# A recommendation tower on one Trainium2 core: in the first tile, when the field-row broadcasts and the second tile's gathers are issued, and where in a tile the embedding conversion stands

## The chip, the cores and the metric

The kernel runs on one core of one Trainium2 chip. The metric is the device time of one execution in microseconds (us), lower is better. Before the change the median of three runs is 2730.25 us (2727.2 to 2735.01).

## The reference, cut to what matters

For each of 2048 samples, 39 ids pick 39 embeddings of 16 numbers. They pass a compressed interaction network of three layers (`_L0_rec_ref`), whose outputs are summed over the 16 numbers; 256 sums and 16 dense features then pass a small multilayer perceptron (272 to 512 to 256 to 1).

```python
e = jnp.stack([tbl_0[ids[:, 0]], ..., tbl_38[ids[:, 38]]], axis=1)
# one layer: x0 is e, xk is the half of the last layer's output that goes on
z = jnp.einsum('bhd,bkd,hks->bsd', x0, xk, W) + b[None, :, None]
z = jax.nn.relu(z)
xk = z[:, :half, :]
direct.append(z[:, half:, :])
# at the end
logit = jnp.sum(jnp.concatenate(direct, axis=1), axis=-1)
```

## The kernel before, in words

**Tiles and chunks.** A tile is 128 samples (16 tiles), and a tile has four chunks of 4 of the 16 embedding numbers, so a chunk is 512 columns. Per tile GpSimd (POOL) gathers 39 embeddings per sample with 39 indirect DMAs (`gather_tile`, L294 to L304) into `emb`. ScalarE (ACT) and VectorE (DVE) convert `emb` into a rounded high part and a remainder (`high_emb` L317, `low_emb` L494, `full_emb` L323) in `emb2`; TensorE (PE) transposes the quarter that a chunk needs (`transposes` L598). ACT copies the transposed rows out of PSUM twice (`copy_x` L328): into `rows_sb`, from which SyncE (SP) writes the chunk's 39 rows to a scratch in DRAM (`write_rows` L233), and into `x2`.

**Layer 0** uses sums of pairs, their squares, and a contraction: seven rounds of `sums` (PE L607), `square` (ACT L337), `contract0` (PE L612). PE and ACT take turns over two PSUM banks, `aux_ready` going from PE to ACT and `aux_read` back. The result becomes `xk1` (`next_field`, L348 and L349).

**Layers 1 and 2** are 20 steps per chunk, numbered k: k 0 to 9 belong to layer 1 and k 10 to 19 to layer 2. Each step takes a pair of field rows, broadcast over 64 partitions each, multiplies it with `xk` on DVE (`product`, L485, 128x1024), and contracts the product on PE. Twelve of the 20 steps are split: ACT rounds the product (L341), DVE forms the remainder (`low`, L490), and PE contracts in three parts (L629, L633). The other eight are plain (L621). The products go through a ring of `RING = 4` buffers, so DVE can be four steps ahead of PE.

**The pairs of rows** come from `spread(c, p)` (L240): two broadcast DMAs of 256 KB each from the DRAM scratch to slot `x_slot(c, p)` of `xb`. Ten pairs serve a chunk, in layer 1 and again in layer 2. The four pairs p < `PRE` = 4 have slots for two chunks, the others one slot. Layer 1 of a chunk starts four steps early: its first four steps are k 6 to 9 of the chunk before, and for chunk 0 of tile 0 a prologue.

**What sets the order.** Each engine runs an instruction list written out by hand, and waits on semaphores. All broadcasts and scratch writes are on SP's one queue. In `tile` (SP, L257) a chunk first writes the rows of the chunk two ahead, and then issues pair p when the product of step k = 10 + p of the chunk has been made. The prologue of SP (L252 to L255) is written as follows:

```python
for c in range(2):
    write_rows(0, c)
    for p in range(PRE if c else PAIRS):
        spread(c, p)
```

So the ten pairs of chunk 0 are issued with no wait between them, and `write_rows(0, 1)` and four pairs of chunk 1 stand behind them. On POOL, `gather_tile(0)` is followed by a loop that waits for `emb2_ready` (the end of the conversion of the tile before) and gathers the next tile; so the gathers of tile 1 start when `full_emb(0)` has ended. PE's and ACT's prologues run layer 0 for group 0 and group 1 (the first two chunks), and inside group 1 the first four steps of chunk 0 (`contract(0, s, ...)`, with `round_` on ACT L369 and the loop of DVE from L516).

**The conversion** of the next tile stands in chunk 1 of every tile but the last, at steps `HIGH_AT, LOW_AT, FULL_AT = 4, 6, 8` (L39): ACT's `high_emb` ahead of its work of step 4, DVE's `low_emb` ahead of step 6, ACT's `full_emb` ahead of step 8. The transposes that need it are at step 0 of chunk 2. Also placed by step number are ACT's `direct2` (3), `next_field` and `direct1` (9), `direct0` (16), `next_field` of layer 0 (19), and DVE's folds, four additions at steps 5 to 8 of chunk 0 and at 12 to 15 of chunk 3.

Of the kernel before, what the change touches and what calls it, by code (L numbers as in the profile page):

```python
# [26 lines left out]
PAIRS = T1 // 2  # L27


PRE = 4  # L30
# [5 lines left out]
SUM_AT = [3, 5, 7, 9, 11, 12, 14]  # L36
SQUARE_LAG, CONTRACT_LAG = 2, 3
RELU2_AT, RELU1_AT, DIRECT0_AT, RELU0_AT = 3, 9, 16, 19
HIGH_AT, LOW_AT, FULL_AT = 4, 6, 8  # L39
FOLD1_AT, FOLD0_AT = 5, 12  # L40
FOLDS = 4
SPL = sorted(SPLIT)
# [12 lines left out]
def step_no(c, k, end=False):  # L55

    return PRE + STEPS * c + k - (PRE if end and k >= L2 else 0)
# [7 lines left out]
def x_slot(chunk, p):  # L65

    return PRE * (chunk % 2) + p if p < PRE else PRE + p


def field(t, j):  # L70

    return NF - 1 if t == SINGLE else 2 * t + j - (2 if t > SINGLE else 0)
# [7 lines left out]
def build(nc, ids, tables, x0_dram, sel0_d, inc_d, w0a_d, w0b_d, w1_d, w2_d, b_d, dense_d, wt1_d, wx_d, bt1_d, wt2_d, bt2_d,  # L80
          wt3_d, out):
    ctx = ExitStack()
    with ctx:
# [6 lines left out]
        def sem(name):  # L90
            return ctx.enter_context(nc.semaphore(name))
# [81 lines left out]
        products = sem("products")  # L173
# [29 lines left out]
        def dram_pair(k):  # L203

            if k >= L2:
                return w2_d[:, 2 * (k - L2):2 * (k - L2) + 2, :]
            p = (k + PRE) % PAIRS
            return w1_d[:, 2 * p:2 * p + 2, :]
# [13 lines left out]
        @block.sync  # L222
        def _(sp):
            sp.dma_start(ids_sb[:, :, :], ids.rearrange("(t p) f -> p t f", p=TB)).then_inc(ids_in, 16)
            for dst, src in ((w0a_st, w0a_d), (w0b_st, w0b_d), (inc, inc_d), (sel0_st, sel0_d),
                             (bias[:, :], b_d), (wt3[:, :], wt3_d), (bt1[:, :], bt1_d), (bt2[:, :], bt2_d)):
                sp.dma_start(dst, src).then_inc(weights_in, 16)
            for q, k in enumerate(SPL):
                sp.dma_start(w_st[:, q], dram_pair(k)).then_inc(weights_in, 16)
            for q, k in enumerate(PLAIN):  # L230
                sp.dma_start(wp[:, q], dram_pair(k)).then_inc(weights_in, 16)

            def write_rows(T, c):  # L233

                sp.wait_ge(rows_ready, T * CPT + c + 1)
                sp.dma_start(x0_dram[c % SCRATCH, 0:NF, :], rows_sb[:, c % 2, :]).then_inc(rows_written, 16)
                sp.wait_ge(rows_written, 16 * (T * CPT + c + 1))
                sp.sem_inc(rows_settled, 1)

            def spread(c, p):  # L240

                q = x_slot(c, p)
                for j in range(2):
                    h, h2 = field(2 * p, j), field(2 * p + 1, j)
                    src = x0_dram[c % SCRATCH, h:h2 + 1:h2 - h, :]
                    sp.dma_start(xb[j * K1:(j + 1) * K1, q, :, :], src.unsqueeze(0).broadcast_to([K1, 2, N]))\
                        .then_inc(xb_in[q], 16)


            sp.wait_ge(weights_made, 6)  # L250
            sp.wait_ge(parts_made, 2)
            for c in range(2):  # L252
                write_rows(0, c)
                for p in range(PRE if c else PAIRS):
                    spread(c, p)  # L255

            def tile(T, last=False):  # L257
                for c in range(CPT):
                    if not (last and c >= 2):
                        write_rows(T, c + 2)  # L260
                    if last and c == CPT - 1:
                        continue
                    for p in range(PAIRS):
                        if last and c == 2 and p < PRE:
                            continue

                        sp.wait_ge(products, T * PER["step"] + step_no(c, L2 + p) + 1)
                        spread(c + 2 if p < PRE else c + 1, p)

            with sp.Fori(0, TILES - 1) as T:  # L270
                tile(T)
            tile(TILES - 1, last=True)


            sp.wait_ge(products, PRE + all_steps - STEPS)
            sp.dma_start(wt1, wt1_d[0:256, :].rearrange("(t p) n -> p t n", p=128)).then_inc(mlp_in, 16)
            sp.dma_start(wt2, wt2_d.rearrange("(t p) n -> p t n", p=128)).then_inc(mlp_in, 16)
            sp.dma_start(wx_st, wx_d).then_inc(mlp_in, 16)

            sp.wait_ge(products, all_steps - (PAIRS - PRE))  # L280
            sp.dma_start(dense_st, dense_d).then_inc(dense_in, 16)
            sp.wait_ge(m3_read, BATCH // N)
            sp.dma_start(out.rearrange("(a n) o -> a (n o)", a=1), y_sb).then_inc(out_done, 16)
            sp.wait_ge(out_done, 16)

        @block.gpsimd
        def _(pool):
            pool.memset(ident[:, :], 0.0).then_inc(idx_ready, 1)
            pool.wait_ge(idx_ready, 1)
            pool.affine_select(out=ident[:, :], in_=ident[:, :], compare_op=ALU.not_equal, fill=1.0, base=0,  # L290
                               pattern=[[-1, 128]], channel_multiplier=1).then_inc(idx_ready, 1)
            pool.wait_ge(ids_in, 16)

            def gather_tile(T):  # L294
                pool.sem_inc(settled, 1)
                pool.tensor_copy(idx[:, :], ids_sb[:, bass.ds(T, 1), :].rearrange("p a f -> p (a f)"))\  # L296
                    .then_inc(idx_ready, 1)
                pool.wait_ge(idx_ready, T + 3)
                pool.sem_inc(settled, 1)
                for f in range(NF):  # L300
                    pool.indirect_dma_start(emb[:, f, :], None, tables[f],  # L301
                                            bass.IndirectOffsetOnAxis(ap=idx[:, f:f + 1], axis=0))\
                        .then_inc(gathered, 16)
                pool.wait_ge(gathered, (T + 1) * (16 * NF))  # L304

            gather_tile(0)
            with pool.Fori(1, TILES) as T:
                pool.wait_ge(emb2_ready, T)
                gather_tile(T)
# [492 lines left out]
```

## Time and profile before

| | us |
|---|---|
| median of 3 runs | 2730.25 |
| the profiled execution | 2730.05 |
| its span | 2728.2 |
| PE busy | 2597.3 (95% of the span) |
| DVE busy | 2471.9 (91%) |
| ACT busy | 1475.9 (54%) |
| POOL busy | 960.2 (35%) |
| 16 DMA engines, queue of SP | 59.3% of their span |

The profiled execution lies 0.2 us under the median, and its span 1.9 us under its own time. Lines such as L485 are lines of the kernel before. In the rows below, "SPq" is the issuing of DMAs by SP; a bracket holds the idle time of the engine ahead of the row and what ended it. "remote" or "another core or an unknown queue" is a semaphore wait whose releaser the profile could not name, and "issue" is time in which the profile shows nothing that the engine waited for. Matmul ends are modelled.

### The profile page before, as it was taken

The page shows a single profiled execution, that of the slowest core. Times are in us where ns is not written, and L with a number is a line of the kernel's source. Part 1 is how long each engine was busy: PE and PEld are TensorE (multiplying, and loading weights), DVE is VectorE, ACT ScalarE, POOL GpSimd, SP SyncE. Part 2 cuts the span into 40 slices and gives each one's busy share as a digit, 9 for nine tenths or more (in the row PEclk, how much of TensorE's full clock was granted, in tenths as well). Part 3 has the DMA queues.
Part 4 walks back from the last instruction along what each step waited for, and adds up shares of the span by engine and source line. Part 5 has one row for each costly group of instructions (what it writes and reads, how often), then busy time and mean ns, then how long its engine had stood idle before and what let it go on. Part 6 is the DMA issues. An engine that isn't in the chain of part 4 may idle for free.

```text
span 2728.2 us, 29051 instructions
## 1 busy us (share of the span) xinstructions
PE 2597.3 (95%) x8334; PEld 1521.9 (56%) x8334; DVE 2471.9 (91%) x2206; ACT 1475.9 (54%) x1863; POOL 960.2 (35%) x646
## 2 busy tenths in 40 slices
PE   1599999999999999999999999999999999999989
PEld 0255565555555555565555555555655555555545
DVE  1299999999999999999999999999999999999991
ACT  1255555655555555555556555555655555555543
POOL 6527071542707153260805326080533608000000
PEclk9799999999999999999999999999999999999999
DMA  2556665675667567566756766675576657556730
GB/s 69 113 117 128 152 140 120 138 159 119 129 147 143 122 132 159 125 131 140 150 122 126 158 129 133 133 156 123 126 151 140 131 124 160 124 126 141 155 77 1
DMA packets 214669, 352.43 MB, mean 129 GB/s; under 512 B 34373, under 2 KB 47546, under 8 KB 214546
## 3 DMA queue, kind: packets, MB, share of 16 engines
q1 hardware_dynamic: 194675, 346.95, 59.3%
q0 software_dynamic: 19968, 5.15, 1.7%
q8 instruction: 14, 0.23, 0.0%
q14 instruction: 12, 0.10, 0.0%
HBM read 346.86 MB, written 5.12 MB: 129 GB/s over the span
## 4 chain that ended last, share of the span: by engine, by line
PE 50%; DVE 23%; issue 15%; DMA 5%; ACT 3%; POOL 1%; another core or an unknown queue 1%; DVEq 1%; SPq 1%; ACTq 0%; POOLq 0%
PE ps L621 16%; PE ps L629 12%; DVE P L485 11%; PE ps L612 9%; DVE Pl L490 9%; PE ps L633 8%; DMA xb<-x_dram 5%; DVE dir L512 2%; PE ps L607 2%; POOL emb L301 1%; ACT Ph L341 1%; PE ps L728 1%; PE ps L718 1%; DVE emb L496 1%
## 5 line engine op out<-in xcount | busy, mean ns | idle before, releaser
L485 DVE TENSOR_TENSOR P<-xb,xk 128x1024 f32<-128x1024 f32 x1280 | 1532.9, 1220 | 48.5 <-issue 21.8
L341 ACT ACTIVATE Ph<-P 128x1024 fp32r<-128x1024 f32 x768 | 807.0, 1057 | 441.9 <-DVE P L485 427.2
L490 DVE TENSOR_TENSOR Pl<-P,Ph 128x1024 fp32r<-128x1024 f32 x768 | 939.2, 1223 | 95.0 <-ACT Ph L341 69.6
L301 POOL DMA_INDIRECT emb<-tbl_in,idx x624 | 883.0, 1415 | 230.2 <-issue 217.0
L621 PE MATMUL ps<-P,wp 128*128 128x512 f32 x2048 | 962.7, 597 | 0.0
L629 PE MATMUL ps<-Ph,wh 128*128 128x512 f32 x1536 | 794.9, 517 | 6.7 <-ACT Ph L341 6.7
L621 PEld LDWEIGHTS ps<-P,wp 128*128 128x128 f32 x2048 | 383.4, 190 | 342.2 <-issue 301.2
L629 PE MATMUL ps<-Ph,wl 128*128 128x512 f32 x1408 | 556.0, 395 | 0.0
L633 PE MATMUL ps<-Pl,wh 128*128 128x512 f32 (+1 forms) x1536 | 517.1, 410 | 30.5 <-DVE Pl L490 28.9
L337 ACT ACTIVATE sq<-ps 117x512 f32<-117x512 f32 (+1 forms) x448 | 264.9, 591 | 459.9 <-PE ps L607 340.3
L612 PE MATMUL ps<-sq,w 117*128 117x512 f32 (+1 forms) x896 | 472.0, 608 | 20.5 <-ACT sq L337 11.3
L296 POOL COPY idx<-ids_sb 128x39 int32 (+1 forms) x16 | 76.6, 4785 | 1131.2 <-ACT emb L325 1127.8
L629 PEld LDWEIGHTS ps<-Ph,wh 128*128 128x128 f32 x1536 | 291.2, 190 | 194.0 <-issue 135.8
L633 PEld LDWEIGHTS ps<-Pl,wh 128*128 128x128 f32 (+1 forms) x1536 | 275.5, 188 | 178.8 <-DVE Pl L490 88.3
L629 PEld LDWEIGHTS ps<-Ph,wl 128*128 128x128 f32 x1408 | 267.7, 190 | 147.1 <-issue 108.2
L607 PE MATMUL ps<-x,sel 78*117 78x512 f32 (+1 forms) x448 | 258.3, 577 | 9.8 <-issue 8.6
L612 PEld LDWEIGHTS ps<-sq,w 117*128 117x128 f32 (+1 forms) x896 | 166.6, 192 | 148.6 <-issue 119.5
L348 ACT ACTIVATE xk<-ps,bias 64x512 f32<-64x512 f32 x128 | 86.7, 677 | 115.8 <-PE ps L612 64.2
L607 PEld LDWEIGHTS ps<-x,sel 78*117 78x117 f32 (+1 forms) x448 | 78.9, 177 | 68.7 <-issue 55.5
L331 ACT ACTIVATE rows_sb<-ps 39x512 f32<-39x512 f32 x64 | 37.9, 592 | 129.4 <-PE ps L600 123.7
L349 ACT ACTIVATE xk<-ps,bias 64x512 f32<-64x512 f32 x128 | 87.3, 682 | 1.6
L600 PE MATMUL ps<-ident,emb 128*78 128x128 f32 x256 | 38.9, 275 | 39.8 <-ACT emb L325 39.8
(53 smaller groups left out, 509.3 us busy)
## 6 DMA issues: line engine op xcount, KB each, us to landing
xb<-x_dram SPq DMA_DIRECT2D x1280, 256.0 KB
emb<-tbl_in,idx POOLq DMA_INDIRECT x624
x_dram<-rows_sb SPq DMA_DIRECT2D x64, 78.0 KB
xb<-w_in SPq DMA_DIRECT2D x12, 128.0 KB
wp<-w_in SPq DMA_DIRECT2D x8, 128.0 KB
xb<-wt_in SPq DMA_DIRECT2D x2, 512.0 KB, 7.1
xb<-dense_in SPq DMA_DIRECT2D x1, 768.0 KB, 5.2
xb<-w0a_in SPq DMA_DIRECT2D x1, 409.5 KB
```

What stands on the lines that cost most here:

```text
L301: pool.indirect_dma_start(emb[:, f, :], None, tables[f], bass.IndirectOffsetOnAxis(ap=idx[:, f:f + 1], axis=0))\
L337: act.activation(sq[0:rows, t % 2, :], aux_ps[0:rows, number % 2, :], ACT.Square).then_inc(aux_read, 1)
L341: act.activation(Ph[:, s % RING], P[:, s % RING], ACT.Copy).then_inc(rounded, 1)
L348: act.activation(xk[lo, :], z[lo], ACT.Relu, bias=b[lo])
L349: act.activation(xk[hi, :], z[lo], ACT.Relu, bias=b[lo]).then_inc(ready, 1)
L485: dve.tensor_tensor(P[:, s % RING], xb[:, slot], xk.unsqueeze(1).broadcast_to([128, 2, N]), ALU.mult)\
L490: dve.tensor_tensor(Pl[:, s % RING], P[:, s % RING], Ph[:, s % RING], ALU.subtract)\
L607: pe.matmul(aux_ps[0:rows, number % 2, :], sel[:, t, 0:rows], x2[0:R2, slot, :], start=True, stop=True)\
L612: m = pe.matmul(z0_ps[bank], w0[0:rows, t, :], sq[0:rows, t % 2, :], start=t == 0, stop=t == T0 - 1)
L621: m = pe.matmul(z, wp[:, PLAIN.index(k), j, :], P[:, s % RING, j, :], start=start and j == 0, stop=stop and j == 1)
L629: pe.matmul(z, w[:, q, j, :], Ph[:, s % RING, j, :], start=start and i + j == 0, stop=False)
L633: m = pe.matmul(z, wh[rows, q, j, :], Pl[rows, s % RING, j, :], start=False, stop=stop and j == 1)
```

## The change

It has three parts.

1. **SP's prologue.** The rows of chunk 0 are written, pairs 0 to 3 of chunk 0 are issued, then the rows of chunk 1 are written; pairs 4 to 9 of chunk 0 follow, each behind a wait for one more product (1 to 6), and pairs 0 to 3 of chunk 1, each behind a wait for one more (7 to 10).
2. **POOL.** Ahead of the loop that gathers tiles 1 to 15 there is a wait for the first product.
3. **The conversion** in chunk 1 of every tile but the last moves from steps 4, 6, 8 to steps 11, 13, 15.

```diff
-HIGH_AT, LOW_AT, FULL_AT = 4, 6, 8
+HIGH_AT, LOW_AT, FULL_AT = 11, 13, 15
...
-            for c in range(2):
-                write_rows(0, c)
-                for p in range(PRE if c else PAIRS):
-                    spread(c, p)
+            write_rows(0, 0)
+            for p in range(PRE):
+                spread(0, p)
+            write_rows(0, 1)
+            for p in range(PRE, PAIRS):
+                sp.wait_ge(products, p - PRE + 1)
+                spread(0, p)
+            for p in range(PRE):
+                sp.wait_ge(products, PAIRS - PRE + p + 1)
+                spread(1, p)
...
             gather_tile(0)
+            pool.wait_ge(products, 1)
             with pool.Fori(1, TILES) as T:
                 pool.wait_ge(emb2_ready, T)
                 gather_tile(T)
```

## Rows read from the trace of the kernel before

**Rows 1.** The page: PE's busy tenths in 40 slices; the group of the gathers

```profile
PE   1599999999999999999999999999999999999989
...
L301 POOL DMA_INDIRECT emb<-tbl_in,idx x624 | 883.0, 1415 | 230.2 <-issue 217.0
```

**Rows 2.** Chain that ended last, 55 to 150 us: start, length, what

```profile
64.68 1.20 PE ps L607 x2
...
76.93 0.68 ACT xk L348
...
78.30 5.65 another core or an unknown queue
...
86.69 1.48 another core or an unknown queue
...
88.80 5.75 issue
...
96.09 7.37 another core or an unknown queue
...
105.02 14.58 another core or an unknown queue
...
129.03 0.68 ACT xk L348
```

**Rows 3.** Timeline of PE around those waits: start, length, instruction

```profile
75.90 0.60 PE L600 MATMUL ps<-ident,emb 128*78 128x128 f32 x4
...
89.97 1.42 PE L607 MATMUL ps<-x,sel 78*117 78x512 f32 x1
...
99.06 0.40 PE L607 MATMUL ps<-x,sel 78*117 78x512 f32 x1
...
108.57 0.41 PE L607 MATMUL ps<-x,sel 78*117 78x512 f32 x1
```

**Rows 4.** By stretch: length, busy PE, PEld, DVE, ACT, POOL; PEclk, DMA share, GB/s

```profile
86.00:90.00 4.00, 3.56 (x7) 1.46 (x6) 0.00 (x0) 1.19 (x2) 3.08 (x4) 0.50 1.07 213
...
110.00:114.00 4.00, 0.00 (x0) 0.00 (x0) 0.00 (x0) 0.00 (x0) 2.74 (x3) 0.75 0.08 6
...
154.00:175.00 21.00, 21.00 (x71) 12.58 (x70) 19.44 (x17) 10.23 (x13) 0.00 (x0) 1.00 1.05 226
```

**Rows 5.** Timeline of SP's DMA issues in tile 0: start, length, instruction

```profile
64.25 0.33 SPq L236 DMA_DIRECT2D x_dram<-rows_sb  x1
66.14 13.54 SPq L246 DMA_DIRECT2D xb<-x_dram  x20
84.59 0.33 SPq L236 DMA_DIRECT2D x_dram<-rows_sb  x1
93.99 9.44 SPq L246 DMA_DIRECT2D xb<-x_dram  x8
...
151.50 18.62 SPq L246 DMA_DIRECT2D xb<-x_dram  x20
```

**Rows 6.** Chunks 1, 2, 3 of one middle tile, then chunk 1 of the last; columns as above

```profile
1126.25:1165.52 39.27, 39.05 (x128) 23.15 (x127) 38.01 (x34) 24.32 (x30) 22.09 (x12) 1.00 0.63 133
1165.52:1204.41 38.89, 38.89 (x128) 23.16 (x127) 37.23 (x33) 22.02 (x28) 24.60 (x19) 1.00 0.69 140
1204.41:1243.19 38.78, 38.78 (x129) 23.30 (x128) 37.72 (x36) 22.00 (x28) 15.85 (x11) 1.00 0.70 144
2551.18:2589.95 38.77, 38.77 (x129) 23.37 (x127) 36.53 (x33) 22.01 (x28) 0.00 (x0) 1.00 0.63 141
```

**Rows 7.** Timeline of DVE and of PE in that middle tile's chunk 1

```profile
1132.35 1.22 DVE L496 TENSOR_TENSOR emb<-emb 128x624 f32<-128x624 f32 x1
...
1149.53 1.26 DVE L490 TENSOR_TENSOR Pl<-P,Ph 128x1024 fp32r<-128x1024 f32 x1
...
1153.14 0.62 PE L633 MATMUL ps<-Pl,wh 128*128 128x512 f32 x2
```

**Rows 8.** Timeline of POOL: the copy of indices ahead of that tile's gathers

```profile
1139.56 5.44 POOL L296 COPY idx<-ids_sb 128x39 int32 x1 [84.49 <-ACT emb L325]
```

## The prediction

> **What bounds the kernel now.** I read the page's slices first, to see where PE, the busiest engine, is not full [rows 1]: from the third slice (a slice is 68 us) to the end it is at nine tenths, and only the first two slices and the very end are lower. PE's work is the same before and after, so there are two places to look: the start, and the small losses of the full stretch.
>
> The start I read in the chain of waits [rows 2]. The reader is to see five pieces between 78.30 and 119.60 us in which no instruction runs on the chain: 5.65, 1.48, 5.75, 7.37 and 14.58 us, 34.8 us in all. Each ends with an instruction of ACT that waits for `aux_ready` from PE. PE had long issued what it waits for [rows 3]: the transposes stand at 75.90 while ACT goes on only at 83.95; the sum of 89.97 is taken up at 103.46, that of 99.06 at 119.60. So PE's signal, or ACT's notice of it, comes many us late, and group 1 takes 50.7 us from 78.30 to the row at 129.03. Group 0, with the same seven rounds, took 12.3 us from 64.68 to 76.93 [rows 2].
>
> What is peculiar to this stretch? At 86 us the DMA engines are full at 213 GB/s [rows 4]. But they are as full in 154 to 175 us, and there PE is busy 21.00 of 21.00 us. The difference is in the queue of SP [rows 5]: here 20 broadcasts are issued in 13.54 us, and the row write at 84.59, behind them, lands only when the next broadcast starts at 93.99. From 66.14 to 93.99 is 27.85 us for 20, or 1.39 us each, so at 79.7 some ten wait in the queue. In steady state 20 are issued over 18.62 us. The gathers of tile 1 run beside them (POOL is busy in both stretches of the start, and not at 154). In the longest hole, at 110 to 114, the broadcasts are gone and only gathers run, at 6 GB/s [rows 4]. So rows point to two suspects, the deep queue and the gathers, and the change thins both.
>
> The full stretch I read by chunks [rows 6]. Chunk 1 of a middle tile takes 39.27 us, chunk 2 38.89, chunk 3 38.78. Chunk 1 of the last tile, which has no conversion, takes 38.77. So 0.50 us of chunk 1 goes with the conversion, in 15 tiles. DVE spends 1.22 us on `low_emb` at 1132.35 [rows 7], ahead of the four split steps 5 to 8, and PE's idle time in that chunk is 39.27 - 39.05 = 0.22 us; the rest shows as matmuls that start later than they could.
>
> **The change part by part.** *SP's prologue.* It removes nothing; twenty-eight broadcasts and two row writes stay. What it moves: the row write of chunk 1 goes from behind 20 broadcasts to behind 8. Eight take 8 x 1.39 = 11.1 us, 66.14 to 77.3, and ACT's rows are there at about 79, so that write no longer queues; a row write alone takes 66.14 - 64.25 = 1.9 us [rows 5]. What it adds: ten waits on SP. The pair for product n (n from 5 to 14) waits for product n - 4, so three products lie between issue and need. The price of a pair, from the rows: 1.9 us for a transfer's round trip and 2 x 1.39 us for the bytes, 4.7 us, and at most 6.0 if its two issues (13.54 / 20 = 0.68 us each) are not covered at all. Three products in the full stretch take 3 x 38.8 / 20 = 5.8 us. I take 4.7, since a pair issued alone has nothing ahead of it, and so put these waits at nothing; the cover is 1.1 us thick. The first four (pairs 4 to 7) are released by the four products of the prologue, long before use. Behind the last wait (product 10) stands the row write of chunk 2; its first reader is the pair released by product 15, five steps or 9.7 us later, against 1.9 us and four pairs of backlog at most, so that costs nothing either.
>
> *POOL.* The gathers of tile 1 start behind product 1, which follows the 78.30 us of the chain [rows 2] by one product of DVE, so at about 80 us, instead of right behind `full_emb(0)`, ahead of 64.68. A tile's 39 gathers take 39 x 1.415 = 55.2 us and their gaps of 0.3 us some 12 [rows 1], behind a copy of at most 5.44 us [rows 8], so they end near 153. The conversion that needs them now stands at step 11 of chunk 1: chunk 0 starts near 99, a chunk lasts at least 38.8, and 11 steps at 1.94 are 21 more, 159 us. So I put this at nothing; it matters through what it takes out of the start.
>
> *The start, summed.* If the holes go, group 1 costs what is left. From below: 50.7 - 34.8 = 15.9 us, if all that PE did under the holes was free. From above: PE worked under three of the holes, from 88.80 to 91.39, 96.09 to 99.46 and 105.02 to 108.98 [rows 3], 9.9 us, which gives 25.8. Group 0 is the nearest row: 12.3 us, with 1.1 for ACT's copies ahead of it, and four contractions on top, of which a chunk's mean is below 1.94 us (38.8 / 20): 21.2. I take 21, for a gain of 50.7 - 21 = 29.7 us (24.9 to 34.8). PE's granted clock was 0.50 of full, the 1.2 GHz level, at 86 to 90 us, after it had idled; a shorter idle may keep the higher level, which I leave in the range.
>
> *The conversion.* Same instructions, other places. What leaves: 0.50 us x 15 = 7.5 us. What comes: at step 13 DVE's remainder is ready at 1149.53 + 1.26 = 1150.79 and PE takes it up at 1153.14 [rows 7], a slack of 2.35 us, more than the 1.22 us of `low_emb`. And chunk 3 carries four folds on DVE at steps 12 to 15 (DVE 37.72 us, with PE full at 38.78 of 38.78) at no cost [rows 6]. ACT's two conversions are 24.32 - 22.02 = 2.3 us in a chunk in which it is busy 24.32 of 39.27. So nothing comes back: gain 7.5 (bounds: 7.5, and a loss of 1.2 a tile if that slack were not there). The gathers of the next tile start seven steps, 13.6 us, later; they leave chunk 1 and reach further into chunk 3. Chunk 2, which has most of them, is 0.12 us over the floor, so I put the shift at nothing, within 0.3 us a tile, 4.5 us either way.
>
> The sum against the profiled execution's own time: 2730.05 - 29.7 - 7.5 = 2692.9, and the median lies 0.2 above it: 2693.
>
> **A rule against the change.** The rows show full DMA engines beside a full PE at 154 us, and full DMA engines beside an ACT that stands still from 88.80 to 94.55 [rows 2, 4]. The Trainium skill (SBUF — State Buffer, "Who interferes with whom") says that DMA never contends with a compute engine and that "PE and ACT never wait on anyone". By that rule the holes aren't made by transfers and thinning them removes nothing; the stretch at 154 us agrees with it, that at 86 does not settle it.
>
> **The rivals.** *The holes stay.* Their cause is something else in this stretch, such as the first pass through the code or the clock; for it speaks that the longest one has idle DMA engines [rows 4], against it that group 0, also a first pass, has none. Only the conversion gains: 2730.25 - 7.5 = 2722.8. The Trainium skill's page SBUF — State Buffer, in the rule above, leads to this case; the trace bears it out at 154 us only, so it has a small chance.
>
> *Half of the holes stay*, because the gathers make them: they still run beside group 1, from 80 us on. For it speaks the 14.58 us hole with gathers alone; against it the middle tiles, where gathers run beside a full PE [rows 6]. 2693 + 34.8 / 2 = 2710.
>
> *The new place costs.* The holes go, but `full_emb` and `low_emb` among steps 13 to 15 take 1.2 us a tile from PE: 2693 + 7.5 + 15 x 1.2 = 2719.
>
> *Slower.* SP's waits are too tight: the lead of three products isn't there, as DVE makes products faster than PE's mean once it has slots, and with ten pairs each waiting the whole 4.7 us DVE stands 47 us. It decides where a pair's landing passes the time of three products. With the gains it ends at 2693 + 47 = 2740, slower than before. If only the excess of 6.0 over 5.8 is lost it is 2 us. Against it: DVE is bounded by PE through the ring of four.
>
> *Less is changed than said.* The waits could be met already when SP comes to them. For pairs 4 and 5 that is so (products 1 and 2 are made at once); for the others not, since product 3 comes behind a rounding in group 1. The short name speaks of the first tile alone, but the third part acts in 15 tiles; it is in the sum.
>
> **How the numbers follow.** Holes gone and conversion free: 0.62, 2693, with 2684 (34.8 us gained, and some of the gathers' 4.5) to 2701. Half the holes: 0.13, 2710. New place costs: 0.06, 2719. Holes stay: 0.12, 2723. Slower: 0.07, around 2740. The likeliest gives 2693. The range reaches over the first three, 2684 to 2720, and leaves out 0.19. A change of under 0.3%, 8.2 us, is about what a measurement here can't tell from none, so faster means under 2722.1 and slower over 2738.4. Faster: the first three and some of the fourth, 0.84. Same: most of the fourth and part of the last, 0.11. Slower: 0.05.
>
> **What would show it.** Right: the chain has no piece named as unknown over 2 us after 78 us; the row `next_field` of group 1 stands near 99 instead of 129.03; middle chunks 1 take 38.8 us. Pair by pair: DVE waits for xb in tile 0 by under 1 us each. Wrong: holes of the old length with PE's sums long done (the cause is another), holes of half the length beside gathers, PE waiting for a remainder at steps 13 to 16 of chunk 1, or DVE's products in chunk 0 of tile 0 each waiting for a broadcast.

## The result and the profile after

The changed kernel takes 2681.49 us, median of 4 runs (2679.7 to 2683.57); the kernel before, run beside it, takes 2728.9 (2727.2 to 2735.01). The ratio is 0.9822, with a 95% interval of 0.9807 to 0.9838: faster by 47 us, which is clear of the noise though under 2%. The forecast was 2693 with a range of 2684 to 2720, so the sign was right and the size was outside the range, 2.5 us below its lower end.

The profiled execution took 2682.74 us, with a span of 2680.9. First the page of the kernel after, as in [rows 1]: PE's slices, and the group of the gathers (busy us, mean ns, idle us ahead).

```profile
PE   0999999999999999999999999999999999999989
...
L307 POOL DMA_INDIRECT emb<-tbl_in,idx x624 | 949.7, 1522 | 226.1 <-issue 212.8
```

The second slice has gone from 5 tenths to 9. The gathers cost more each, 1522 ns for 1415 in [rows 1], and nothing on the chain waits for it. The chain of waits of the kernel after, in the stretch of [rows 2] (start, length, what):

```profile
77.34 0.68 ACT xk L356
78.04 0.59 ACT rows_sb L338
...
79.17 0.79 PE ps L614
79.98 0.60 ACT sq L344
...
93.83 1.72 PE ps L628 x4
95.55 0.86 PE ps L619 x2
...
96.85 2.82 issue
```

Between 78 and 96.4 us no piece is named "unknown" any more: ACT and PE hand over to each other, and `next_field` of group 1 begins at 96.44 where it began at 129.03. The timeline of the kernel after, SP's issues in tile 0 and this row of ACT (start, length, instruction, idle time ahead of it):

```profile
66.23 5.22 SPq L246 DMA_DIRECT2D xb<-x_dram  x8
...
78.66 0.33 SPq L236 DMA_DIRECT2D x_dram<-rows_sb  x1
80.50 28.25 SPq L246 DMA_DIRECT2D xb<-x_dram  x20
...
96.44 0.68 ACT L355 ACTIVATE xk<-ps,bias 64x512 f32<-64x512 f32 x1 [2.85 <-PE ps L619]
...
108.98 0.39 SPq L236 DMA_DIRECT2D x_dram<-rows_sb  x1
```

The burst of [rows 5] is now 8 broadcasts, then the row write, which lands in 1.84 us (78.66 to 80.50), then 20 broadcasts over 28.25 us. The four chunks of the middle tile (columns of [rows 4]):

```profile
1045.68:1086.79 41.11, 39.86 (x128) 22.84 (x127) 40.74 (x38) 22.03 (x28) 0.00 (x0) 1.00 0.60 134
1086.79:1125.57 38.78, 38.78 (x129) 23.32 (x128) 37.85 (x34) 24.50 (x30) 9.47 (x7) 1.00 0.63 133
1125.57:1164.34 38.77, 38.77 (x128) 23.30 (x127) 37.17 (x33) 22.01 (x28) 32.67 (x21) 1.00 0.68 138
1164.34:1203.11 38.77, 38.77 (x128) 23.30 (x127) 37.85 (x36) 22.11 (x28) 21.59 (x14) 1.00 0.69 137
```

Against [rows 6], chunk 1 has lost 0.49 us and chunk 2 0.12; over all tiles chunk 2 lost 0.26 on average. The chunks' lengths over all tiles, from the starts of PE's transposes in the two timelines, divide the whole difference of the spans:

| | before, us | after, us | gained |
|---|---|---|---|
| start of the first full chunk | 128.83 | 96.25 | 32.6 |
| chunks 0, sum | 661.2 | 659.7 | 1.5 |
| chunks 1 | 589.3 | 581.6 | 7.7 |
| chunks 2 | 585.6 | 581.6 | 4.0 |
| chunks 3 | 586.3 | 584.8 | 1.5 |
| end | 177.06 | 177.04 | 0.0 |
| sum | | | 47.3 |

Two thirds of the gain is at the start, one third in the steady state (how much of that third a second pair of profiles repeats is told below). The row of 41.11 us is worth a look as well: chunk 0 is 2.3 us longer than the others, before and after.

### The profile page after: what moved, and what is told of

Same layout as the page of the kernel before. It is cut to its first block, busy times and chain, and to the rows that moved or that the text cites. A ratio compares the mean times of both kernels' runs of the same rounds, so it can differ in the third digit from the quotient of the medians.

```text
span 2680.9 us, 29052 instructions
## 1 busy us (share of the span) xinstructions
PE 2582.5 (96%) x8334; PEld 1524.9 (57%) x8334; DVE 2468.8 (92%) x2206; ACT 1480.1 (55%) x1863; POOL 967.0 (36%) x646
## 4 chain that ended last, share of the span: by engine, by line
PE 69%; DVE 15%; issue 9%; DMA 4%; POOL 1%; ACT 1%; DVEq 0%; SPq 0%; ACTq 0%; POOLq 0%
PE ps L628 24%; PE ps L636 18%; PE ps L619 12%; PE ps L640 10%; DVE P L492 7%; DVE Pl L497 5%; DMA xb<-x_dram 4%; PE ps L614 3%; DVE dir L519 2%; POOL emb L307 1%; PE ps L735 1%; PE ps L725 1%; PE ps L607 1%; ACT Ph L348 0%; SPq L246 0%
## 5 line engine op out<-in xcount | busy, mean ns | idle before, releaser
L307 POOL DMA_INDIRECT emb<-tbl_in,idx x624 | 949.7, 1522 | 226.1 <-issue 212.8
L302 POOL COPY idx<-ids_sb 128x39 int32 (+1 forms) x16 | 16.6, 1038 | 1096.1 <-ACT emb L332 1070.4
```

What stands on the lines that cost most here:

```text
L307: pool.indirect_dma_start(emb[:, f, :], None, tables[f], bass.IndirectOffsetOnAxis(ap=idx[:, f:f + 1], axis=0))\
```

## The experiments

One thing has to be known ahead of the numbers. The kernel before was run on seven occasions, the comparison above among them. It took about 2730 us on three (2728.9, 2731.66, 2731.80) and about 2697 on the other four (2697.47, 2698.42, 2696.06, 2699.93); its runs of one occasion lie within 9 us. The same chip number stands on record for 2698.42 and for 2731.80, so the chip alone doesn't decide it. Each measurement is read against the kernel before of its own occasion. "The waits" below are the five pieces of [rows 2], which the prediction calls holes, and waits like them. The edits are cut, and shown against the kernel after; the column of parts says what else a run has. "Start" is the time at which chunk 0's first full pass begins in the profile, in us.

| run | parts of the change, folds | this, us | before beside it | ratio (95%) | start |
|---|---|---|---|---|---|
| sp_only | 1 | 2698.61 | 2697.47 | 1.0003 (0.9994 to 1.0013) | 96.34 |
| pool_only | 2 | 2700.54 | 2697.47 | 1.0009 (1.0000 to 1.0019) | 94.12 |
| steps_only | 3 | 2683.79 | 2697.47 | 0.9944 (0.9927 to 0.9960) | 93.91 |
| order_only | 1, no SP waits | 2697.80 | 2697.47 | 0.9999 (0.9989 to 1.0008) | 92.38 |
| before_again | none | 2698.52 | 2698.42 | 0.9997 (0.9987 to 1.0006) | 94.1 |
| after_again | 1, 2, 3 | 2684.44 | 2698.42 | 0.9940 (0.9923 to 0.9956) | 95.87 |
| late_gathers | 1, 2, gathers held | 2694.33 | 2698.42 | 0.9984 (0.9974 to 0.9994) | 94.07 |
| fold12 | 1, 2, 3, folds 12 | 2656.14 | 2698.42 | 0.9838 (0.9822 to 0.9854) | 94.07 |
| oldstart_fold14 | 3, folds 14 | 2652.99 | 2696.06 | 0.9842 (0.9824 to 0.9860) | 94.65 |
| sp_steps_fold12 | 1, 3, folds 12 | 2654.83 | 2696.06 | 0.9845 (0.9829 to 0.9862) | 94.57 |
| pool_steps_fold12 | 2, 3, folds 12 | 2655.02 | 2696.06 | 0.9848 (0.9831 to 0.9864) | 96.00 |
| sp_steps_fold14 | 1, 3, folds 14 | 2680.86 | 2731.66 | 0.9817 (0.9788 to 0.9845) | 122.77 |
| pool_steps_held | 2, 3, folds 14, gathers held | 2654.45 | 2731.66 | 0.9720 (0.9692 to 0.9748) | 93.9 |
| gath_rows | gathers at 68 us, 3, folds 12 | 2654.42 | 2699.93 | 0.9834 (0.9805 to 0.9862) | 94.13 |
| gath_split | 13 gathers at 63 us, 3, folds 12 | 2653.36 | 2699.93 | 0.9830 (0.9801 to 0.9859) | 94.0 |
| gath_rows_b | as gath_rows | 2654.09 and 2691.01 | 2731.80 | 0.9786 (0.9707 to 0.9864) | 94.22 |
| best | 2, 3, folds 14 | 2654.20 | 2731.80 | 0.9719 (0.9703 to 0.9736) | 93.2 |

### One part at a time

**sp_only**: the change's part 1 alone.

```diff
-HIGH_AT, LOW_AT, FULL_AT = 11, 13, 15
+HIGH_AT, LOW_AT, FULL_AT = 4, 6, 8
...
-            pool.wait_ge(products, 1)
```

> The kernel before with part 1 alone (SP's prologue with its ten waits); gathers of tile 1 start at once, conversion at 4, 6, 8. Theory A (the holes come from the deep queue of broadcasts): all five holes go, next_field of group 1 at 96 to 98 us, time 32 us under before, about 2697. Theory B (the gathers make them): half or more of the 34.8 us stay, next_field of group 1 at 110 us or later, time 2712 or more. Chunks 1, 2 and 3 stay at 39.28, 39.03 and 39.06 us in both.

**pool_only**: part 2 alone, with SP's prologue of the kernel before.

```diff
-HIGH_AT, LOW_AT, FULL_AT = 11, 13, 15
+HIGH_AT, LOW_AT, FULL_AT = 4, 6, 8
...
-            write_rows(0, 0)
-            for p in range(PRE):
...
+            for c in range(2):
+                write_rows(0, c)
+                for p in range(PRE if c else PAIRS):
+                    spread(c, p)
```

> The kernel before with part 2 alone (POOL waits for product 1); 20 broadcasts still issued in one burst. Theory A: the holes stay within a few us, next_field of group 1 after 120 us, time 2725 to 2730. Theory B: they go wholly or mostly, time about 2697 to 2712. A hole of 14.58 us that had gathers alone beside it should at least shrink if gathers have a part in it.

**steps_only**: part 3 alone; SP's and POOL's lines as before.

```diff
-            pool.wait_ge(products, 1)
...
+            for c in range(2):
+                write_rows(0, c)
+                for p in range(PRE if c else PAIRS):
+                    spread(c, p)
```

> The kernel before with part 3 alone (conversion at 11, 13, 15). The start is that of before (next_field of group 1 at 129 us). The prediction's term was 7.5 us in chunk 1 and nothing elsewhere: 2722. The trace of after shows 7.7 in chunk 1, 4.0 in chunk 2, 1.5 each in chunks 3 and 0; if all of that is this part's, the time is 2730 - 14.7 = 2715, and chunk 2 is at 38.77 us.

**order_only**: the row write of chunk 1 goes ahead of pairs 4 to 9, but no pair waits for a product.

```diff
             for p in range(PRE, PAIRS):
-                sp.wait_ge(products, p - PRE + 1)
                 spread(0, p)
             for p in range(PRE):
-                sp.wait_ge(products, PAIRS - PRE + p + 1)
                 spread(1, p)
```

> The kernel before with SP's prologue reordered (row write of chunk 1 ahead of pairs 4 to 9) but with no waits for products; POOL and conversion as before. The 20 broadcasts of pairs 4 to 9 and of chunk 1 are now issued in one burst at about 80 us. Theory A in the form 'a burst of 20 is too deep': the holes come back, perhaps later by one group, and the time is within 10 us of before. Theory A' (what hurts is the row write queued behind the burst, with SP standing at its wait): holes go, about 2697. Theory B: as before.

On this occasion the kernel before took 2697.47 us, and no profile of the four has the waits: chunk 0 starts at 92.4 to 96.3 us in all of them. So these runs say nothing on what removes the waits. They say what is left without them: parts 1 and 2 and the mere order of SP gain nothing (1.0003, 1.0009, 0.9999), and part 3 alone gains 13.7 us. pool_only has a cost of its own in tile 0: its conversion at step 4 of chunk 1 waits for gathers that begin late, and that chunk takes 42.88 us instead of 39.3. Parts 2 and 3 belong together.

### Both kernels again, and where the steady state gains

**before_again**: the kernel before, without an edit, with a profile of its own.

> The kernel before, unchanged, with a profile of this occasion. The runs of before beside sp_only, pool_only, steps_only and order_only took 2697.5 us, 33 under the first ones. Theory C: the five holes at 78 to 120 us do not belong to the kernel but come and go with the occasion; where before takes 2697, its group 1 ends near 94 to 96 us, with no wait by an unknown releaser over 1 us, and where it takes 2730 the holes are there. Theory A or B (the program's own queue or gathers make them every time): the holes are in this profile too, and the time is 2728 to 2732.

It took 2698.52 us, as the kernel before beside it. Its timeline, SP's issues and a row of ACT:

```profile
66.22 13.16 SPq L246 DMA_DIRECT2D xb<-x_dram  x20
79.42 0.56 SPq L236 DMA_DIRECT2D x_dram<-rows_sb  x1
...
94.30 0.68 ACT L348 ACTIVATE xk<-ps,bias 64x512 f32<-64x512 f32 x1 [2.85 <-PE ps L612]
94.41 5.12 SPq L246 DMA_DIRECT2D xb<-x_dram  x8
```

and its stretch of [rows 4]:

```profile
86.00:90.00 4.00, 4.00 (x16) 2.65 (x15) 3.74 (x5) 2.04 (x3) 3.08 (x4) 1.00 1.06 215
```

This is the most telling profile of the study. The queue is as deep as in [rows 5], 20 broadcasts in 13.16 us with the row write behind them for 15 us; the DMA share is 1.06 at 215 GB/s; four gathers run beside it. And PE is busy 4.00 of 4.00 us at a clock of 1.00, where in [rows 4] it had 3.56 at 0.50, and group 1 ends at 94.30 instead of 129.03. So neither the deep queue nor the full DMA engines make the waits by themselves, and the late row write costs nothing. The gathers of tile 1 run beside group 0 here too, from 63.68 us, so on this occasion they don't make the waits either.

**after_again**: the changed kernel, without an edit.

> The kernel after, unchanged, on the same chip as before_again. Theory C: 2680 to 2684 as the first time, since its start has no holes either way; the ratio to before is 0.994 (15 us) where before takes 2697. Theory A or B: ratio 0.982.

2684.44, 3 us over its first time, beside a before that is 30 us under its own. Chunks 1 and 2 take 38.77 us again, and chunk 0 starts at 95.87, 1.8 us *later* than in before_again. That isn't the change's: late_gathers and fold12 below have the same start program and begin chunk 0 at 94.07. What differs is the granted clock in group 1. It is 0.50 at 80 to 84 us and 0.70 at 84 to 86 in after_again, and in before_again 0.54 and 0.61 at 80 to 84 and 1.00 from 84. The change's worth is 14 us where the waits don't occur (0.9940), and 47 where they do.

**late_gathers**: the changed kernel with the conversion back at steps 4, 6, 8, while the gathers of tiles 2 to 15 are held until the product of step 15 of chunk 1. It parts the two things that part 3 moves.

```diff
-HIGH_AT, LOW_AT, FULL_AT = 11, 13, 15
+HIGH_AT, LOW_AT, FULL_AT = 4, 6, 8
...
             pool.wait_ge(products, 1)
-            with pool.Fori(1, TILES) as T:
+            pool.wait_ge(emb2_ready, 1)
+            gather_tile(1)
+            with pool.Fori(2, TILES) as T:
                 pool.wait_ge(emb2_ready, T)
+                pool.wait_ge(products, T * PER["step"] - 120)
                 gather_tile(T)
```

> The kernel after, but with the conversion back at 4, 6, 8, and the gathers of tiles 2 to 15 held until the product of step 15 of chunk 1 (about where full_emb ends in after). Splits part 3 into its two effects. If the conversion's place gives chunk 1's 0.5 us a tile and the later gathers give chunk 2's 0.27: chunk 1 at 39.28, chunk 2 at 38.77, time 7.5 us over after plus some 3.5 for gathers of tile 1 that are late for step 4: 2692. If chunk 2's gain is DVE's lead from the new place: chunk 2 at 39.03, 2696. If chunk 1's 0.5 us is the gathers': chunk 1 at 38.77.

Its chunks 1, 2 and 3 of the middle tile:

```profile
1092.44:1131.78 39.34, 39.10 (x129) 23.16 (x128) 38.00 (x34) 24.29 (x30) 10.79 (x8) 1.00 0.63 134
1131.78:1170.55 38.77, 38.77 (x128) 23.31 (x127) 37.03 (x33) 22.01 (x28) 32.67 (x21) 1.00 0.69 138
1170.55:1209.67 39.12, 39.12 (x129) 23.08 (x128) 37.65 (x36) 21.98 (x28) 18.97 (x13) 1.00 0.68 141
```

Chunk 1 is back at 39.3 although the gathers are late, and chunk 2 stays at 38.8 although the conversion is early. So the half microsecond of chunk 1 belongs to the place of the conversion, and what chunk 2 gained belongs to the later gathers. The waits of DVE from 130 to 2507 us (us in total, times, longest) point the same way. In before_again and in after_again:

```profile
DVE P L485 <- DMA xb<-x_dram: 30.3, 51, 1.4
```

```profile
DVE P L492 <- DMA xb<-x_dram: 12.8, 22, 1.5
```

DVE's waits for broadcasts fall from 30.3 to 12.8 us (21.5 to 7.5 in the first pair of profiles), and to 15.2 in late_gathers, with later gathers alone. steps_only, with part 3 alone, has 13.4. In the kernel before the gathers of the next tile begin at step 8 of chunk 1, beside the burst of its later pairs; that this overlap is what lengthens DVE's waits is argued, not shown.

### The folds

Chunk 0, at 41.11 us with DVE at 40.74, has four folds of DVE at steps 5 to 8, the same kind of place from which the change took `low_emb`. **fold12** puts them at steps 12 to 15; the rest is the changed kernel.

```diff
-FOLD1_AT, FOLD0_AT = 5, 12
+FOLD1_AT, FOLD0_AT = 12, 12
```

> The kernel after with the folds of chunk 0 moved from steps 5 to 8 to steps 12 to 15, where chunk 3 has its own at no cost. Chunk 0 takes 41.0 us against 38.8 for chunks 1 and 2, with PE waiting for remainders at steps 5 to 8. By the same reading as for the conversion: chunk 0 falls to 38.8 to 39.0 in 15 tiles, 30 to 34 us, time 2648 to 2652. If chunk 0's excess is not the folds' (the loop's branch, or broadcasts of the chunk before): it stays at 41.0 and the time at 2681.

Its chunks 0 and 1 of the middle tile:

```profile
1037.02:1076.01 38.99, 38.99 (x128) 23.04 (x127) 38.99 (x37) 22.11 (x28) 0.00 (x0) 1.00 0.61 137
1076.01:1114.98 38.97, 38.97 (x128) 23.16 (x127) 38.97 (x34) 24.62 (x30) 9.36 (x7) 1.00 0.63 135
```

2656.14, 28.3 us under after_again. All chunks 0 together go from 660.8 to 629.2 us, a gain of 31.6, and chunks 1 give back 2.5 (581.6 to 584.1), where DVE is now busy without a pause. [rows 6] show 38.77 us as the length of an undisturbed chunk; chunk 0 is 0.2 over it now. The prediction used four folds at steps 12 to 15 of chunk 3 as proof that late steps have slack, and overlooked the four in chunk 0 that stood at early ones.

### Which part removes the waits

**oldstart_fold14**: part 3 with folds at step 14, SP and POOL as before.

```diff
-FOLD1_AT, FOLD0_AT = 5, 12
+FOLD1_AT, FOLD0_AT = 14, 12
...
+            for c in range(2):
+                write_rows(0, c)
+                for p in range(PRE if c else PAIRS):
+                    spread(c, p)
...
-            pool.wait_ge(products, 1)
```

> The kernel before with part 3 and with chunk 0's folds at steps 14 to 17; SP's and POOL's starts as before. If the start parts cost 1.8 us where there are no holes (chunk 0 began at 94.1 us in before_again and at 95.9 in after_again): 1 to 2 us under fold12's 2656, and if steps 14 to 17 hide the folds fully (fold12: chunk 0 at 38.97, chunk 1 at 38.93, floor 38.77), another 5 us: 2649 to 2655. If before takes 2730 on this occasion, theory C2 (the occasion and the old start together make the holes) gives this kernel them too: 2682 to 2688; theory C1 (the occasion alone, whatever the start, and after was lucky) gives them to all three kernels of this call or to none.

**sp_steps_fold12**: the changed kernel without part 2, folds at 12.

```diff
-FOLD1_AT, FOLD0_AT = 5, 12
+FOLD1_AT, FOLD0_AT = 12, 12
...
-            pool.wait_ge(products, 1)
```

> Parts 1 and 3 and the folds at 12; POOL's start as before. Without holes: 2655 to 2657, as fold12. If before takes 2730 here: theory A (queue) no holes, 2656; theory B (gathers) holes, 2672 or more.

**pool_steps_fold12**: without part 1, folds at 12.

```diff
-FOLD1_AT, FOLD0_AT = 5, 12
+FOLD1_AT, FOLD0_AT = 12, 12
...
+            for c in range(2):
+                write_rows(0, c)
+                for p in range(PRE if c else PAIRS):
+                    spread(c, p)
```

> Parts 2 and 3 and the folds at 12; SP's start as before. Without holes: 2654 to 2657; chunk 0 starts at 94.1 us if the 1.8 us are the waits of SP, at 95.9 if they are those of POOL. If before takes 2730 here: theory A holes, 2672 or more; theory B none, 2656.

2652.99, 2654.83 and 2655.02: again an occasion without the waits, and the three can't be told apart. So they don't say which part removes the waits; they repeat that the start is worth nothing then. The next two came on an occasion on which the kernel before took 2731.66.

**sp_steps_fold14**: parts 1 and 3, folds at 14.

```diff
-FOLD1_AT, FOLD0_AT = 5, 12
+FOLD1_AT, FOLD0_AT = 14, 12
...
-            pool.wait_ge(products, 1)
```

> Parts 1 and 3, the folds of chunk 0 at 14 to 17; POOL's start as before. If before takes 2697 here: 2652 to 2656. If it takes 2730: theory A (holes need the burst of broadcasts of the old start) 2652 to 2656, theory B (they need the gathers of tile 1 beside group 1) 2670 or more with holes in the chain after 78 us.

**pool_steps_held**: parts 2 and 3, folds at 14, and the gathers of tiles 2 to 15 held to step 4 of chunk 2.

```diff
-FOLD1_AT, FOLD0_AT = 5, 12
+FOLD1_AT, FOLD0_AT = 14, 12
...
+            for c in range(2):
+                write_rows(0, c)
+                for p in range(PRE if c else PAIRS):
+                    spread(c, p)
...
+            pool.wait_ge(emb2_ready, 1)
+            gather_tile(1)
+            with pool.Fori(2, TILES) as T:
                 pool.wait_ge(emb2_ready, T)
+                pool.wait_ge(products, T * PER["step"] - 111)
                 gather_tile(T)
```

> Parts 2 and 3, folds at 14 to 17, and the gathers of tiles 2 to 15 held until step 4 of chunk 2, when the broadcasts of chunk 1's second half have landed. Chunk 3 is still 0.2 us over the floor in after, with DVE waiting for broadcasts that ran beside gathers. If only overlap with a burst counts: chunk 2's burst and chunk 3's are now beside gathers, so chunk 3 stays at 39.0 and chunk 0 rises by 0.2: 2656. If before takes 2730 here: theory A 2670 or more with holes, theory B none.

2680.86 against 2654.45: 26 us between them, and their starts are 122.77 and 93.9. Chain of sp_steps_fold14 (start, length, what):

```profile
76.35 2.12 issue
...
82.10 2.72 issue
...
92.03 21.52 another core or an unknown queue
...
115.11 3.44 another core or an unknown queue
...
122.97 0.68 ACT xk L354
```

Its timeline, rows of POOL, SP, PE and ACT:

```profile
63.42 0.96 POOL L307 DMA_INDIRECT emb<-tbl_in,idx  x1 [0.81 <-POOL idx L302]
...
65.96 5.26 SPq L246 DMA_DIRECT2D xb<-x_dram  x8
...
79.95 41.14 SPq L246 DMA_DIRECT2D xb<-x_dram  x12
...
95.10 0.39 PE L613 MATMUL ps<-x,sel 78*117 78x512 f32 x1
...
113.57 0.60 ACT L343 ACTIVATE sq<-ps 117x512 f32<-117x512 f32 x1 [21.54 <-remote]
114.22 2.07 PE L618 MATMUL ps<-sq,w 117*128 117x512 f32 x2 [18.72 <-issue]
```

PE's sum stands at 95.10, and ACT squares its result at 113.57: the picture of [rows 3], with SP's queue as shallow as the change makes it, and gathers from 63.42 on. The trace also has the moment at which PE's signal arrives. The sum ends at 95.50, the event of its semaphore stands at 113.55, and ACT goes on 0.02 us later; in before_again such an event stands 0.01 to 0.02 us behind the matmul's end. So it is the signal that is late, not ACT's notice of it. And the timeline of pool_steps_held, rows of SP, POOL and ACT:

```profile
66.20 13.02 SPq L246 DMA_DIRECT2D xb<-x_dram  x20
...
80.04 0.97 POOL L301 DMA_INDIRECT emb<-tbl_in,idx  x1 [0.81 <-POOL idx L296]
...
94.10 0.68 ACT L352 ACTIVATE xk<-ps,bias 64x512 f32<-64x512 f32 x1 [2.85 <-PE ps L616]
```

The old burst of 20, gathers from 80.04 on, and no wait. The two kernels differ in SP's prologue and in the hold of later tiles as well, but all four pairings of the two parts are on record for the three occasions. With gathers from 63 us the waits are there under the old prologue (the kernel before) and under the new one (sp_steps_fold14); with gathers from 80 us or later they are gone under both (the kernel after; this run, and best below without the hold). So on such an occasion POOL's line removes the waits, and SP's part neither removes them nor is needed. The hold itself gains nothing: chunk 2 is short already, and chunk 0 is 39.12 us.

**gath_rows** lets the gathers of tile 1 begin once the first row write has landed, at 67.7 us, so inside group 0. **gath_split** issues 13 of them at once, from 63.5 us, and 26 behind product 1. Both have part 3, folds at 12 and SP's old prologue.

```diff
-            pool.wait_ge(products, 1)
+            pool.wait_ge(rows_settled, 1)
```

> pool_steps_fold12 with POOL waiting not for product 1 (about 78 us) but for the first row write to have landed (about 66 us): the gathers of tile 1 start some 3 us later than before's 62.6 and run through half of group 0 and all of group 1. Where before takes 2697: 2653 to 2657. Where it takes 2730: if any start during group 0 brings the holes, 2670 or more; if only gathers that begin before PE's group 0 do, 2655.

```diff
+                    if split and f == 13:
+                        pool.wait_ge(products, 1)
...
-            pool.wait_ge(products, 1)
+            gather_tile(1, split=True)
```

> pool_steps_fold12 with the first 13 gathers of tile 1 issued at once (62.6 to 79 us) and the other 26 behind product 1. In the first trace of before the first hole began at 78.3, with the 13th gather. Where before takes 2697: 2653 to 2657. Where it takes 2730: if gathers in group 0 bring the holes later on, 2670 or more; if it takes an unbroken row of more than 13, 2655.

2654.42 and 2653.36 beside a before of 2699.93: once more an occasion without the waits, so nothing is told on them. **gath_rows_b** is gath_rows again.

> gath_rows once more, for an occasion on which before takes 2730: 2670 or more if gathers that start in group 0 bring the waits, 2655 if they don't. Where before takes 2697: 2653 to 2657, and nothing is learned.

This time the kernel before took 2731.80, and the two executions took 2654.09 and 2691.01 us. The profile is that of the first. It has one short wait of the kind, in its chain (start, length, what):

```profile
84.36 2.74 another core or an unknown queue
...
87.12 0.60 ACT sq L338
```

The sum that ACT squares there ends at 85.21, and its signal comes at 87.10. The second execution, 37 us longer, was not profiled. So a start of the gathers inside group 0 still lets PE's signals come late; that the 37 us are such waits is an inference from their size.

**best**: parts 2 and 3 with folds at steps 14 to 17, SP as before.

```diff
-FOLD1_AT, FOLD0_AT = 5, 12
+FOLD1_AT, FOLD0_AT = 14, 12
...
+            for c in range(2):
+                write_rows(0, c)
+                for p in range(PRE if c else PAIRS):
+                    spread(c, p)
```

> Parts 2 and 3, chunk 0's folds at 14 to 17, SP's old start: the version to keep. 2651 to 2656 whatever before takes, since POOL's part is enough against the waits of the start and the old SP start was 1.3 us faster in oldstart_fold14 and sp_steps_fold12 (chunk 0 at 94.6 us).

2654.20 (2653.12 to 2655.22), 77.6 us under the kernel before of that occasion: it beats both kernels, and it has no new wait on SP. Its chunks 0 and 1:

```profile
1033.81:1072.81 39.00, 39.00 (x129) 23.09 (x128) 39.00 (x37) 22.19 (x28) 0.00 (x0) 1.00 0.64 138
1072.81:1111.82 39.01, 39.01 (x129) 23.21 (x128) 39.01 (x34) 24.60 (x30) 9.29 (x7) 1.00 0.64 132
```

Its gathers of tile 1 are issued from 80.7 to 146 us, beside most of group 1 and of chunk 0, and its start is at 93.2. So gathers beside matmuls don't make the waits as such; the waits come with gathers that begin ahead of or beside group 0, on some occasions.

## Why the prediction was right and wrong

**The holes go** (right, by the wrong part). The chain has no unknown piece from 78 us on, as the first mark for "right" asked. But the prediction named two suspects and leaned on the deep queue of SP. before_again has that queue and no holes, and sp_steps_fold14 has the shallow queue and holes. The gathers were the second suspect, and moving them was what helped. The rival that blamed them expected half of the holes to stay, since gathers still run beside group 1; none stayed, so what counts is when they begin, not that they run beside it. Two other causes that the prediction named don't hold. No packet of an instruction queue is in the trace of the kernel before from 68 to 127 us, so no code was loaded under the holes. And the granted clock was still 1.00 at 78 to 80 us, when the first hole began, and fell behind it; before_again has 0.54 at 80 to 82 and no hole.

**What group 1 costs without holes** (a term mis-sized). "I take 21, for a gain of 50.7 - 21 = 29.7 us". Group 1 took 18.4 us, from 78.04 to 96.44, so 32.6 us were gained at the start, inside the bounds of 24.9 to 34.8. The four contractions were priced at a mean step, 7.8 us together; in the chain after they take 5.9 us, three of 1.38 and the last of 1.72 (93.83), and the rest of group 1 takes 12.5 us where 13.4 was put. PE didn't keep its clock: in the kernel after it idled for 2.12 us ahead of 79.17, and was granted 0.50, the 1.2 GHz level, at 80 to 84 us, 0.58 at 84 to 86 and 1.00 from 86. In order_only and best it was 1.00 all through, and chunk 0 started at 92.38 and 93.2.

**That the holes belong to the kernel** (not seen). All rows came from one profile. Four of seven occasions have no holes, and no row of a single profile could have told that. The change is worth 14 us on one kind of occasion and 47 on the other. That the comparison fell on the second kind, as the profile before had, is luck: on the first kind the forecast of 2693 would have stood beside a kernel before of 2697 and a kernel after of 2684.

**SP's waits cost nothing** (right). DVE's products of chunk 0 in tile 0 don't wait for a broadcast, and the pairs of 80.50 to 108.75 keep ahead. The slower rival (0.07) had no part. The 1.8 us by which after_again starts later than before_again aren't theirs, as the two runs with the same start program at 94.07 show.

**The row write** (right). It no longer queues, and as before_again shows, its queueing had cost nothing.

**The gathers of tile 1** (right). They ran from 81.3 to 144.6 us, forecast 80 to 153, ahead of step 11 of chunk 1. pool_only shows the cover that the prediction named: with the conversion at step 4 that chunk is 3.6 us longer. The copy ahead of the gathers had a median of 5.44 us before [rows 8] and has 1.12 after.

**The conversion** (right in size). 7.5 us was forecast for chunk 1, and 7.7 came; late_gathers shows that it is its place. Nothing came back at steps 11 to 15: PE is busy 38.78 of 38.78 us.

**The later gathers** (the step that failed). "Chunk 2, which has most of them, is 0.12 us over the floor, so I put the shift at nothing". One middle tile stood for fifteen: over all tiles chunk 2 was 0.26 over the floor, and 4.0 us came from there. It repeats: the chunks 2 sum to 585.6 and 585.7 us in the two profiles of the kernel before, and to 581.6 and 581.8 in the two after. Chunks 3 and 0 gave 1.5 each in this pair of profiles, but two profiles of one kernel differ as much there (chunks 3: 586.3 and 587.7 before, 584.8 and 585.9 after; chunks 0 after: 659.7 and 660.8), so those 3.0 us aren't shown to be the change's. With 2.9 more from the start and 0.2 from chunk 1 this is 10.1 us more than the sum of the prediction; its sum said 2693, and the profiled execution took 2682.74. So two terms failed in size, the shift of the gathers (0 for 4.0) and group 1 (21 for 18.4), both inside their own bounds. The lower end of the range, 2684, took the start's bound whole and the gathers' only in part, and had nothing for chunks 3 and 0.

**The rule against the change.** By the Trainium skill's rule (SBUF — State Buffer, "Who interferes with whom"), DMA never contends with a compute engine. That agrees with before_again, where PE is busy all 4.00 us beside full DMA engines. The prediction drew from it that thinning would remove nothing; that step failed, since the later start of the gathers did remove the waits. The rule itself isn't refuted: it and its sentence "PE and ACT never wait on anyone" are about ports of SBUF, and what ACT waited for was a signal of PE, up to 18.1 us behind the end of the matmul (sp_steps_fold14).

**What stays open.** What delays PE's signals. In sp_steps_fold14 the last gather is issued at 111.88 and the long wait ends at 113.57; in the first profile the last gather is at 112.4 and the last wait ends at 119.60. The ends stand near each other, but they don't name a mechanism. Nor do the runs say what makes an occasion one or the other. One mark of it is in the traces. In the six of the three occasions with the waits, those of the kernel after and of best among them, 456 to 483 events of PE's `aux_ready` are recorded where PE signals 512 times; in the thirteen others it is 505 to 513. So on such an occasion records of signals are missing even where no signal is late, and whether late signals and missing records have one cause, the recording itself included, no run here shows.

## What to carry to other kernels

Look in an unrolled schedule for small operations that stand ahead of a run of the most demanding steps, and move them to where slack is: here 0.5 us per tile for one conversion and 2 for four additions, 36 us together, more than the whole stall at the start. Before a start-up stall is costed, profile the unchanged kernel on another occasion: here it was there three times in seven, and a gain of 47 us is 14 without it. Try a later start for the bulk gathers of a later tile: here they cost up to 33 us when they began beside the first stage, on some occasions, and 4 us when they began seven steps earlier in chunk 1.

## What the runs showed of the hardware

The same program took 2697 or 2730 us by occasion, with its runs of one occasion within 9 us of each other, and the difference is about that of the waits for PE's signals between 78 and 120 us. On the occasions with the waits, they were in both profiles whose gathers begin at 63 us (the kernel before, sp_steps_fold14), a single short one of 2.76 us in the profile whose gathers begin at 67.5 (gath_rows_b), and none in the three whose gathers begin at 80 or later (the kernel after, pool_steps_held, best). In a wait PE's signal is recorded up to 18.1 us (sp_steps_fold14) and 20.1 us (the kernel before, 99.46 to 119.60) behind the matmul's end. Without a wait, one start program began chunk 0 between 93.2 and 96.0 us (pool_only, pool_steps_fold12, best), with a granted clock of 1.00 throughout group 1 in best and of 0.50 at 80 to 84 in pool_steps_fold12. A POOL copy of 128x39 integers took 0.21 us where DVE was idle (tile 1's, in the start), and by median 5.44 or 1.12 us at its two places in the full stretch. A gather took 0.94 us or 1.96 in the same chunk, so the mean of 1415 ns hides two prices.
